# A graph network's first step reordered, and its edge state loaded plainly and turned by TensorE instead of by a transposing load

## The reference

```python
edge_attr = swish(edge_attr_raw @ enc_W + enc_b)
for _ in range(4):
    e_in = concatenate([edge_attr, x[src], x[dst]], axis=-1)
    e_upd = layernorm(swish(e_in @ eW1 + eb1) @ eW2 + eb2, eg, ebeta)
    edge_attr = edge_attr + e_upd
    agg = segment_sum(edge_attr, dst, num_segments=3125)
    n_in = concatenate([x, agg], axis=-1)
    x = x + layernorm(swish(n_in @ nW1 + nb1) @ nW2 + nb2, ng, nbeta)
out = layernorm(x0 + x)          # no gain, no bias
```

## Time and profile before

| | |
|---|---|
| median of 3 runs | 3197.7 us (3197.43 to 3201.09) |
| the profiled execution | 3224.33 us, its span 3222.6 us |
| PE, DVE, ACT, POOL busy | 81%, 65%, 58%, 47% of the span |
| mean granted clock of PE | 0.947 |
| last releaser chain | PE 73%, issue 14%, DVE 8% |
| first step's edge slots | about 112 to 930 us |
| later steps' edge slots | 1043 to 1667, 1775 to 2403, 2514 to 3145 us |

### The profile page before, as it was taken

The page is one execution under the profiler, slowest core; times in us unless marked ns, Lnnn a source line. Parts: engine busy times, 40 slices in busy tenths (PEclk is TensorE's granted clock), DMA queues, the critical chain, the costliest instruction groups (busy, mean ns, idle before and its releaser), DMA issues.

```text
span 3222.6 us, 82752 instructions
## 1 busy us (share of the span) xinstructions
PE 2595.9 (81%) x27702; PEld 1937.5 (60%) x27702; DVE 2090.2 (65%) x6292; ACT 1869.0 (58%) x5337; POOL 1518.2 (47%) x1581
## 2 busy tenths in 40 slices
PE   3778888888896888888887788888887788888886
PEld 1456666666673666666674566666664566666665
DVE  5566667777774566666674466666675466666667
ACT  2556566666653666666663566666664466666664
POOL 0544454544412555555521555555530655555540
PEclk9888888899898999999999999999999899999998
DMA  3544444444425788777744677787754666666650
GB/s 105 154 131 140 135 134 141 142 142 142 142 85 139 184 200 202 204 202 207 203 138 139 168 205 204 198 205 203 204 156 124 152 166 160 164 159 164 165 135 21
DMA packets 649002, 512.86 MB, mean 159 GB/s; under 512 B 363436, under 2 KB 560178, under 8 KB 648568
## 3 DMA queue, kind: packets, MB, share of 16 engines
q1 hardware_dynamic: 573304, 301.83, 36.6%
q0 software_dynamic: 75264, 205.62, 22.2%
HBM read 312.28 MB, written 117.85 MB: 133 GB/s over the span
## 4 chain that ended last, share of the span: by engine, by line
PE 73%; issue 14%; DVE 8%; ACT 1%; DMA 1%; another core or an unknown queue 1%; DVEq 1%; POOL 1%; ACTq 0%; SPq 0%; POOLq 0%
PE psum L1632 19%; PE psum L1613 14%; PE psum L1602 12%; PE psum L1663 7%; PE psum L1644 6%; PE psum L1594 5%; PE psum L1382 3%; PE psum L2040 2%; DVE arena L1851 2%; PE psum L2079 2%; PE psum L2053 1%; DVE arena L1825 1%; PE psum L1659 1%; DVE arena L1862 1%
## 5 line engine op out<-in xcount | busy, mean ns | idle before, releaser
L1571 POOL DMA_INDIRECT arena<-node_tables,idx_all x1568 | 1515.6, 967 | 1606.6 <-remote 555.1
L1815 DVE SCALAR_TENSOR_TENSOR arena<-psum,arena 128x1024 f16<-128x1024 f32 x392 | 479.2, 1223 | 666.8 <-issue 571.6
L1726 ACT ACTIVATE arena<-psum 128x1024 f16<-128x1024 f32 x392 | 401.5, 1024 | 848.0 <-PE psum L1613 460.6
L1632 PE MATMUL psum<-w_hi,arena 128*128 128x128 f16 x6272 | 675.2, 225 | 130.4 <-issue 122.4
L1632 PEld LDWEIGHTS psum<-w_hi,arena 128*128 128x128 f16 x6272 | 516.0, 101 | 262.5 <-issue 218.2
L1602 PE MATMUL psum<-ident,arena 128*128 128x128 f16 x6272 | 507.2, 222 | 166.9 <-issue 148.1
L1632 PE MATMUL psum<-w_lo,arena 128*128 128x128 f16 x3136 | 591.2, 225 | 40.3 <-issue 37.4
L1602 PEld LDWEIGHTS psum<-ident,arena 128*128 128x128 f16 x6272 | 402.3, 99 | 248.9 <-issue 217.1
L1749 ACT ACTIVATE arena<-psum 128x128 f32<-128x128 f32 x1568 | 412.8, 278 | 199.7 <-remote 160.0
L1851 DVE SCALAR_TENSOR_TENSOR arena<-arena,psum 128x128 f32<-128x128 f32 x1568 | 482.3, 340 | 6.1 <-remote 2.6
L1613 PE MATMUL psum<-arena,w_hi 128*128 128x512 f16 x1568 | 481.7, 389 | 5.5 <-issue 5.5
(11 more groups left out here) (169 smaller groups left out, 2730.7 us busy)
## 6 DMA issues: line engine op xcount, KB each, us to landing
state<-arena SPq DMA_DIRECT2D x294, 256.0 KB
arena<-node_tables SPq DMA_DIRECT2D x784, 64.0 KB
arena<-matrices SPq DMA_DIRECT2D x294, 128.0 KB
node_tables<-arena SPq DMA_DIRECT2D x100, 256.0 KB, 2.2
arena<-node_tables,idx_all POOLq DMA_INDIRECT x1568
arena<-rel_rows SPq DMA_DIRECT2D x98, 128.0 KB
matrices<-arena SPq DMA_DIRECT2D x98, 128.0 KB
arena<-state SPq DMA_TRANSPOSE x294
```

Of the source, the lines that this page charges most:

```text
L1571: pool.indirect_dma_start(out=rows[n % R][:, t, :], out_offset=None, in_=p_table, in_offset=bass.IndirectOffsetOnAxis(ap=idx_all[:, n % G1 ...
L1632: x = pe.matmul(ps_v(k2)[:, t * P:(t + 1) * P], h[k2][:, half, t * P:(t + 1) * P], w[:, half, :], start=False, stop=half == 1 and h is hl, ...
L1726: act.activation(hh[k2], ps_h(k2), ACT.Silu).then_inc(S("hh"), 1)
L1815: dve.scalar_tensor_tensor(hl[k2], ps_h(k2), 1.0, hh[k2], ALU.mult, ALU.subtract).then_inc(S("hl"), 1)
```

## The change

In the first step PE encodes at the end of its slot, after `node_sums`, and no longer between `hidden` and `output`. On DVE, in all steps, `add_window` stands at the head of the slot and serves group `n - 8` instead of `n - 7`; the loop has one slot more at its end.

In the later steps SP loads the state plainly, edges on the partitions, into `st_in` (eight buffers), once `new` of eight groups ago is there. PE turns it with eight transposes into fp16 in the PSUM bank `ps_t` (`turn`, a slot ahead), ACT copies the 1024 columns to `eT` (two buffers), and `hidden` reads `eT`. `turn_back` is gone there; `scale` adds the low part of the state from SBUF, and one more DVE instruction, `add_old`, adds the high part. ACT seeds no bias in the later steps: PE does it with a matmul of 512 columns for every group.

```diff
@@ SP
-                    sp.wait_ge(S("turned"), n - RE + 1)
+                    sp.wait_ge(S("turned") if n - RE < G1 else S("new"), n - RE + 1)
-                    sp.dma_start(turned_in[n % RE].rearrange("f k (t e) -> f (k t) e", t=TPG),
-                                 state[n % G1, :, :], transpose=True).then_inc(S(f"st{n % RE}"), 16)
+                    sp.dma_start(st_in[n % RE].rearrange("p k e -> p (k e)"), state[n % G1, :, :]).then_inc(S(f"st{n % RE}"), 16)
@@ PE
                     if s:
-                        pe.wait_ge(S(f"st{n % RE}"), 16 * (self.ring(n, RE) - self.before(n % RE, RE)))
+                        pe.wait_ge(S("eT"), n - G1 + 1)
+                def turn(n):
+                    if not first <= n <= last or s == 0:
+                        return
+                    pe.wait_ge(*self.loaded(n))
+                    if n > G1:
+                        pe.wait_ge(S("eT"), n - G1)
+                    for p in range(2):
+                        for t in range(TPG):
+                            m = p * TPG + t
+                            x = pe.transpose(ps_t[:, m * P:(m + 1) * P], st_in[n % RE][:, p, t * P:(t + 1) * P], ident16[:, :])
+                    x.then_inc(S("transposed"), 1)
                 def output(n):
-                    if BIAS_ACT and n - first >= 2:
-                        pe.wait_ge(S("seed"), n - 2 * s - 1)
+                    if s == 0 and n >= 2:
+                        pe.wait_ge(S("seed"), n - 1)
+                turn(first)
                 for n in range(first, last + 1):
                     hidden(n)
-                    encode(n + 2)
+                    turn(n + 1)
                     if n > first:
                         output(n - 1)
                     turn_back(n - LAG)
                     node_sums(n - LAG - 3)
+                    encode(n + 2)
@@ ACT
+                def turned(n):
+                    if not first <= n <= last or s == 0:
+                        return
+                    act.wait_ge(S("transposed"), n - G1 + 1)
+                    if n - 2 >= G1:
+                        act.wait_ge(S("h"), n - 1)
+                    act.copy(eT[n % 2], ps_t[:, :].rearrange("c (k e) -> c k e", k=2)).then_inc(S("eT"), 1)
                 for n in range(first, last + 1):
                     silu(n)
-                    encode_silu(n + 2)
-                    seed(n)
+                    turned(n + 1)
                     if n > first:
                         squares(n - 1)
                     high(n - LAG - 1)
-                    encode_high(n + 2)
+                    if s == 0:
+                        encode_silu(n + 2)
+                        seed(n)
+                        encode_high(n + 2)
@@ DVE
+                def add_old(n):
+                    if not here(n) or s == 0:
+                        return
+                    dve.wait_ge(S("scaled"), n - G1 + 1)
+                    dve.scalar_tensor_tensor(e_new[n % R], e_new[n % R], 1.0, st_in[n % RE][:, 0, :],
+                                             ALU.mult, ALU.add).then_inc(S("new"), 1)
                 def slot(n):
-                    w = window(n - LAG - 3)
+                    add_window(n - LAG - 4, window(n - LAG - 4))
                     matrices_of(n + 2)
                     first_low(n + 1)
                     low(n)
```

43 lines of the change are left out of this document (25 added, 18 removed).

## The result

The changed kernel takes 3011.9 us (3010.8 to 3012.5, four runs) where the kernel before takes 3197.6 us on the same chip: a ratio of 0.942, 95% interval 0.940 to 0.944. The direction was forecast; the size, -186 us instead of -33, lies outside the range. The profiled execution has a span of 3010.4 us. The ratios compare fast executions alone and are not always to the last digit the quotient of the two medians beside them.

What follows compares the result with a forecast made beforehand. The prediction saw the first step bound by a PE-DVE ring, later steps by PE's work plus stops at POOL's gathers. First step -99, bias +63, step ends +3 gave -33 us: 3197.7 to 3165 us, range 3095 to 3290.

Steps and rivals of the forecast that it cites:

- The bound of the later steps: Later slots: PE's 4.86 us of work plus two stops of 0.8 us at POOL's paired gathers make 6.48 us.
- First step, -99 us: First step: some 86 slots fall from 8.6 to 7.45 us, -99 us (bounds -120 to -77).
- the ring: First step: PE's node sums, DVE's add_window, scale and gains, PE's encode mid-slot, node sums again; slot 8.6 us.
- both holds: First step: two losses of 0.8 us a slot on PE while POOL gathers, lifting 6.1 us of work to 7.7.
- both edges of the ring are cut: First step: add_window takes a sum made a slot earlier, and encode wants its gu at the slot's end.
- Bias, +63 us: Later steps, PE: one more 512-column matmul of 0.215 us in 294 slots, +63 us if nothing hides it; bounds 0 and +63.
- Ends of steps, +3 us: Step tails: one more DVE slot in each, about 1 us each, +3 us.
- Turning by PE, copy by ACT, SP: 0: Later steps: eight transposes replace turn_back's matmuls, ACT's copy has 0.7 us slack, the plain load lands early; each 0.
- DVE, 0: Later steps: add_old costs 0.68 us, DVE rises from 4.3 to 5.0 us of a 6.7 us slot; cost 0.
- Rival A: Later steps: turned tile reaches hidden's six state matmuls late, +87 to +204 us, 3252 to 3369 us; chance 0.27.
- Rival B: Later steps: the transposing load causes one or both PE stops; dropping it gives 2930 or 2700 us; chance 0.09.
- Rival C: First step: ACT's new chain ends late before output, slot 8.05 us, gain 47 instead of 99, 3217 us; chance 0.12.

Runs made afterwards that it cites:

- stops_none: Kernel before with POOL's gathers of the later steps left out after each step's first four groups: 2776.6 us against 3230.2, ratio 0.859.
- more_pe: Kernel before with the eight matmuls of turn_back done twice in the later steps: 3266.6 us against 3232.0, ratio 1.011.
- bias_by_act: Changed kernel with the second layer's bias seeded by ACT in the later steps too: 3052.6 us, ratio 0.945, against the changed kernel's 0.943.
- k2_encode: Kernel before with only the first step's encoding matmuls, and ACT's encoding silu and seed, moved: 2595.0 us, ratio 0.958, where the kernel before takes about 2714.
- k2_again: Kernel before with only the first step's encoding move, on a chip where the kernel before takes 3232.0 us: 3045.4 us, ratio 0.943.
- k12_noadd: Changed kernel with DVE's add_old cut from 512 columns to 8 in the later steps: 3039.9 us, ratio 0.941.
- stops_plain: Kernel before with a plain load of the old state instead of the transposing one: ratio 0.998 on a slower chip, 0.992 on a faster one.
- k5_transposing: Changed kernel with the transposing load in place of its plain load of the old state: 2654.3 us, ratio 0.981.
- k6_actbias: Changed kernel with the bias seeded by ACT in the later steps too, on a faster chip: 2649.1 us, ratio 0.979.
- after_again: The changed kernel unaltered, on a chip where the kernel before takes 2714.6 us: 2648.9 us, ratio 0.978.

## Why the prediction was wrong

**The bound of the later steps.** That PE's own work is 4.86 us, that the stops stand at the gathers' ends and that signals are seen late was right (`stops_none`). What failed is the use that was made of "So PE's own work is 4.86 us, and 1.62 us a slot are lost": the loss was taken as a fixed term that adds to PE's work wherever POOL gathers, so that each edit on PE counted in full, in the first step too. `more_pe` (35 us, not 131) and `bias_by_act` (0, not 63) show that the sum does not hold on this kind of chip: a later slot stays at some 6.3 to 6.6 us with 4.86, 5.08 or 5.31 us of PE's work in it. It behaves like the larger of PE's work and two bursts of two gathers with their pauses; that the gathers' own cycle sets the other length is argued, not shown.

**First step, -99 us.** Right: the ring, that the change cuts it, that PE is next. The step that failed, and that most of the miss comes from, is "With both holds, 1.6 us, 7.7", which led to 7.45 us a slot (bounds 7.2 and 7.7). Measured: 6.59 us over the step, 6.24 in undisturbed stretches, which is PE's work alone; PE idles 0.34 us a slot in all, and most of that is not a hold but ACT's seed. With 6.4, between these two, the sum had read 86 x (8.6 - 6.4) = 189 us, near the 178 found. The lower bound rests on a misread row: the early slots of 6.5 us "with holds" do hold 5.4 us of work, but the two stops that the waits of PE list in them, 1.6 and 0.4 us, stand in front of the encoding, inside no row, and the longer one ends when DVE's L1825 is done (149.11 us). From the chain of the kernel before:

```profile
147.64 1.61 issue
149.25 1.09 PE psum L1382 x2
```

Eight sums and four counts more then need not lengthen the slot by their 0.67 us. Also wrong was "both edges of the ring are cut" as the reason: one edge is enough (`k2_encode`, `k2_again`). And the prediction has no term for the clock: its slot of 8.6 us contains PE's work at 1.2 GHz, worth some 68 us over the step. That did not spoil the sum, since the measured slot had it in and the new one was worked out from rows at 2.4 GHz, but a reader who adds up PE's waits alone finds only 109 of the 178 us.

**Bias, +63 us.** Mis-sized, the lower bound of 0 is what was measured, on both kinds. The argument against hiding it ("leaves nothing to spare in 6.48 less two stops of 0.8") took what a slot loses for fixed. The displayed stops are no shorter (0.44 and 0.52 us against 0.41 and 0.51), but a slot less PE's own work is 1.25 us here (6.33 - 5.08), and 1.4 on the other chips of the kind, against 1.62 before.

**Ends of steps, +3 us.** Too small: each of the three later steps starts some 6 us later, as said above, 18 to 19 us together. In the changed kernel's trace the wait for ACT's copy stands at these three starts; what delays the first copy was not looked into.

**Turning by PE, copy by ACT, SP: 0.** Right within a step. The six state matmuls wait for the copy three times in 294 slots, once at the start of each later step, 39.8 us in total (the waits of the changed kernel: us, times, the longest):

```profile
PE psum L1615 <- ACT arena L1789: 39.8, 3, 13.5
```

**DVE, 0.** Right on the first kind (`k12_noadd`), probably wrong on the second, where DVE is at 92% in a later slot. The prediction set DVE's 5.0 us against a slot of 6.7; against PE's own 4.86 us, the slot without stops, it would have stood out.

**Rival A** (tile late, slower) did not come: those three waits are all there is at its place, and none is inside a step. The Trainium skill (Perfetto Trace Analysis, Optimization Strategy) counts a gap repeated on the engine that should be saturated as a possible want of buffers; here going from eight turned tiles to two did not widen the two stops, and the gap goes with the gathers (`stops_none`). **Rival B** is refuted (`stops_plain`). The Trainium skill (Advanced Engine Details and Errata, X-Bar Transpose) has transposing DMAs as fast as plain ones; the kernel's time agrees with that within 8 us of 3230 on the first kind, while on the second the plain load saves 21 us. The transfers themselves differ in the traces: the packets of the queue that carries the load take 46.6% of the DMA engines' span with the transposing load (`k5_transposing`) and 35.1% with the plain one (`k6_actbias`, same chip, 2654.3 and 2649.1 us). **Rival C** (first step stays near 8) came only in part: its sign, PE waiting before `output` for ACT's seed, is there, with 20.3 us in 23 slots on the first chip, where it had set 52 us; on the second kind (`after_again`) there is none.

**The range.** Its upper part was spent on A. Below, it was also too narrow by the prediction's own bounds: -120 + 0 + 3 us makes 3081, and -77 + 63 + 3 makes 3187, not "3125 to 3205". The measured 3012 lies outside all of them. No case held "no stops in the first step", though the trace of before had the sign: next to none stood inside PE's rows there.

The better kernel is `k2_encode`, the old one with the encoding's move alone: 2595.0 us where the changed kernel takes 2648.9 on the same chip, and the same ratio on the first kind.

## What to carry to other kernels

When an engine loses time regularly, ask whether the loss adds to its work or leaves the slot as long as it was: a run with some work added, and one with some taken away, tell which, and until then a price for a small edit on that engine is a guess between nothing and the whole. Do not carry a loss from one stretch to another without finding it in the rows of the second. Where an engine's waits go with a lower granted clock, removing them gains more than the waits themselves, here 178 us for 109. In a ring across engines, look first for the one in-order request that sits in the middle of a full engine's slot; moved to the end, it may make the other edges harmless. And an engine that costs nothing under a stalled slot is to be compared with the slot without the stall: that is where another chip may run.

## What the runs showed of the hardware

The kernel before takes 3198 to 3232 us on four chips and 2714 us on two, with a granted clock of 0.94 to 0.95 on the former and 0.96 to 0.97 on the latter. Most of the difference goes with the gathers of the later steps: without them a later slot is 4.86 us on both kinds, and 159 of some 516 us remain (2776.6 against 2618.0), most of them in the old first step. On the first kind a burst of POOL's gathers is followed by a pause of 0.9 to 2.0 us until PE's signals are seen, ACT idles 1.5 to 1.8 us in front of its silu instead of 0.8, and PE stops inside a row of matmuls that waits for nothing. On the second kind POOL pauses 0.30 us, and PE's rows have no such stops. Single gathers 2.2 to 2.6 us apart hardly bring it on the first kind either (a mean slot of 5.0 us). What in the chip makes it is open; the runs show only what it goes with.

In the first step the granted clock was 0.90 where PE waited 1.5 us or more in many slots, and 0.99 with these waits gone; the same matmuls kept PE busy for 674.5 and 606.2 us.
